# Reordering the drains of two local-attention stages, and the statistics and products around them

## The chip, the cores and the metric

The kernel runs on one core of a Trainium2 chip. The metric is the device time of one execution in microseconds, here the median of several runs. The engines are PE (TensorE), DVE (VectorE), ACT (ScalarE), POOL (GpSimd) and SP (the queue that issues the DMAs).

## The reference

A token mixer, one layer of linear attention and two layers of local attention with a gated feed-forward, all in 32-bit floats. The feed-forward layers see 4096 tokens of 256 channels.

```python
h = einsum('bhid,oi,od->bho', x, weighted_sum, weight)      # images to 4 x 512 tokens
h = concatenate([h, txt], axis=1)                           # 4 x 1024 tokens of 256
h = h + linear_attention(layernorm(h))                      # 16 heads of 64, elu+1, gate
x = layernorm(h)
for l in range(2):
    qkv = shift_token(x) @ wqkv[l]                          # 8 heads of 64
    q, k = rotary_xpos(l2norm(q) * qs, l2norm(k) * ks)
    x = x + local_attention(q, k, v) @ wo[l]                # windows of 128, the one before seen too
    g = layernorm(shift_token(x)) * ln_g + ln_b
    a, b = split(g @ w1[l] + b1[l], 2)
    x = x + (a * gelu(b)) @ w2[l] + b2[l]                   # hidden 682
h = h + x
```

`shift_token` takes the second half of the channels from the token before.

## The kernel before

The 4096 tokens are 32 tiles of 128 (`T = 32`). Every product of 32-bit operands is made of three matmuls (`matmul3`, lines 117 to 119): each operand is split into a rounded high part (a copy by ACT) and the rest (a subtraction by DVE). The program is a sequence of blocks, and at the end of each block all engines meet: `tok_phase`, `attention_phase`, and then `local_phase` and `mlp_phase` for each of two layers. Inside a block each engine has its own list of instructions, written out by hand, and semaphores (`Count`) tie the lists. A `wait(count, n)` holds the whole engine, and everything behind it on that engine.

**Attention.** Four batches of eight tiles. In each batch DVE works out the mean and the variance for the next batch (`norm.variance`, eight small chained instructions, lines 157 to 164), takes the summed key-value products out of PSUM (`take_kv`, line 711), and PE may start the gate projections only when that is done. In batch 0 alone DVE also makes the low part of the output weights in one instruction (line 764), before `take_kv`. At the end of the last batch PE transposes the gated output of the last tile (line 1047), projects window 1 of the first local layer (`qk(1)`, twelve matmuls of 512 columns), makes two output products of 24 matmuls each, and warms itself with ten transposes of the identity (`keep_warm`, line 125). DVE's last work in the block is `bn_stats` on the last two tiles of `H` (line 846).

**Local attention.** A software pipeline over steps `n`: step `n` projects window `n`, scores window `n - 1`, transposes and applies the probabilities of window `n - 2`, and makes the output product of window `n - 3`. Steps 1 to 3 are written out, then a loop, then the drain `T`, `T + 1`, `T + 2`, in which ever less is left. In layer 0, DVE does the variance of the last eight tiles after step 2 and the inverse root (ten small instructions and one more) after step 3 (`between`); ACT waits for it before the loop. In each step ACT makes eight exponentials (line 1317) with their row sums, DVE inverts the sums (line 1453), and POOL multiplies the probabilities by them in two halves of four heads (line 1264). POOL also adds and scales the rotated queries and keys (lines 1272 and 1142).

In the drain, DVE makes the statistics of the first feed-forward group of four tiles in step `T` (`first_stats`) and its eight normalising instructions in step `T + 1` (`first_norm`, lines 1414 and 1416), right after the low part of the attention output (line 1457). PE transposes the result at the end of step `T + 1` (line 1658). Behind the last step DVE scales it by `ln_g` and `ln_b` (line 1529), ACT rounds it (line 1376) and DVE takes the low part (line 1534).

**Feed-forward.** Eight groups of four tiles. For each of six pieces `c` of the hidden layer: `up` (twelve matmuls of 512 columns), gelu on ACT, product `u` on DVE (line 1909), `u_hi` on ACT, `u_lo` on DVE (line 1919), `down`. DVE first has to make the statistics of group 1 (lines 1874 and 1880), for which the shifted channels of group 1 are read back from DRAM. It then works through `hidden(0)`, variance, `hidden(1)`, inverse root, the product of `hidden(2)` and `normalise`, and PE transposes group 1 (line 2010) after that.

Of the kernel before, what the change touches and what calls it, by code (L numbers as in the profile page):

```python
# [12 lines left out]
P = 128  # L13
# [4 lines left out]
T = B * TB  # L18
# [386 lines left out]
def attention_phase(nc, s, mem, K, A):  # L405
# [62 lines left out]
    with nc.Block() as block:  # L468
# [152 lines left out]
        def _(dve):  # L621
# [108 lines left out]
            def batch(b, first, last):  # L730
# [113 lines left out]
            dve.wait_ge(*s.attn_t_done.after(t_full + 6))  # L844
            for w in range(2):
                nc.vector.bn_stats(K.h_stats[:, T - 2 + w], H[:, T - 2 + w])

        @block.tensor
        def _(pe):
# [191 lines left out]
            fill = fills(B - 1, True)[0](STAGES, 0)  # L1041
            pe.wait_ge(*s.attn_o.after(OB * B))
# [6 lines left out]
            qk(1)  # L1049
# [89 lines left out]
def scaled_window(nc, t1, rn, a):  # L1139

    v = t1[:, a].rearrange("p (h d) -> p h d", d=DH)
    return nc.gpsimd.tensor_tensor(v, v, rn[:, a * LH:(a + 1) * LH].unsqueeze(2).to_broadcast([P, LH, DH]), ALU.mult)  # L1142


def local_phase(nc, s, mem, K, A, layer):
# [43 lines left out]
    with nc.Block() as block:  # L1189
# [56 lines left out]
        def _(pool):  # L1246
# [11 lines left out]
            def normalise(t):  # L1258

                pool.wait_ge(*s.inverted.after(t + 1))  # L1260
                for half in range(2):
                    heads = slice(half * LH // 2, (half + 1) * LH // 2)
# [19 lines left out]
            with pool.Fori(2, T // 2) as p:  # L1282
# [4 lines left out]
                nc.gpsimd.tensor_tensor(K.w_l[:, piece], K.w_raw[:, piece], f32(K.w_h[:, piece]), ALU.subtract)  # L1287
                window(2 * p + 1)
            for t in (T - 2, T - 1):
                normalise(t)  # L1290

        @block.scalar
        def _(act):
# [38 lines left out]
            def step(n, r, a, b, c, d, piece=None):  # L1332
# [23 lines left out]
                if a:  # L1356
# [3 lines left out]
                    x_hi(n + 1, 1 - r)  # L1360
                if c:
# [12 lines left out]
            for c in range(KC):  # L1374
                act.wait_ge(*ms.hf.after(c + 1))
                nc.scalar.activation(m_nh[0][:, c], m_hf[:, c], ACT.Copy).then_inc(ms.n_hi.sem, 1)

        @block.vector
        def _(dve):
# [30 lines left out]
            def first_norm():  # L1410

                wait(dve, s.v_full, T)
# [22 lines left out]

            def one_of(n, *steps):
# [3 lines left out]
            def step(n, r, a, b, c, d):  # L1440
# [9 lines left out]
                if c:  # L1450
# [35 lines left out]
                for h in range(LH):  # L1486
# [6 lines left out]
                    if a:  # L1493
# [3 lines left out]
                        else:  # L1497
                            rnorm(LAST).then_inc(s.rnorm.sem, 1)

            late = TB * (B - 1)  # L1500

            def between(n):

                if layer == 0 and n == 2:
                    K.tile_stats(late, T).variance(nc, chain)
                if layer == 0 and n == 3:
                    K.tile_stats(late, T).deviation(nc, chain)
                    nc.vector.scalar_tensor_tensor(nmr[:, late:T], K.l_mean[:, late:T], -1.0, rs[:, late:T], ALU.mult,
                                                   ALU.mult).then_inc(s.stats.sem, 1)
# [17 lines left out]
            for c in range(KC):  # L1527
                dve.wait_ge(*ms.n_t.after(c + 1))
                nc.vector.tensor_scalar(m_hf[:, c], ps[:, c], K.lg[:, layer, c:c + 1], K.lb[:, layer, c:c + 1],
                                        ALU.mult, ALU.add).then_inc(ms.hf.sem, 1)  # L1530
            last_add()
            for c in range(KC):
                dve.wait_ge(*ms.n_hi.after(c + 1))
                nc.vector.tensor_tensor(m_nl[0][:, c], m_hf[:, c], f32(m_nh[0][:, c]), ALU.subtract).then_inc(ms.n_lo.sem, 1)

        @block.tensor
        def _(pe):
# [55 lines left out]
            def step(n, r, a, b, c, d):  # L1593
# [60 lines left out]
                if drain(n, 1):  # L1654
                    pe.wait_ge(*ms.normed.after(1))
                    for c in range(KC):
# [851 lines left out]
```

## Time and profile before

| | us |
|---|---|
| median of 3 runs | 1815.03 |
| lowest and highest | 1814.41, 1819.37 |
| the profiled execution | 1819.65 |
| its span, first to last instruction | 1817.9 |
| PE busy | 1771.5 (97%) |
| DVE busy | 1395.9 (77%) |
| ACT busy | 1003.8 (55%) |
| POOL busy | 528.0 (29%) |

Times in the rows of the trace are microseconds from the first instruction. The local stages lie at about 625 to 1018 (layer 0) and 1221 to 1616 (layer 1). A busy PE is not one at its best, since matmuls overlap: a matmul of 512 columns is listed with 0.39 us, and the next starts 0.23 us after it. The clock column is the granted clock of TensorE as a share of its upper level of 2.4 GHz.

### The profile page before, as it was taken

The numbers are of one execution on the slowest core, as the hardware profiler recorded it, in microseconds if no ns is written. First come the engines' busy times: TensorE is split into PE (matmuls) and PEld (weight loads), VectorE is DVE, ScalarE is ACT, GpSimd is POOL, SyncE is SP. The second block draws the span as 40 slices with busy tenths as digits, with TensorE's granted clock in tenths as the row PEclk, the third lists the DMA queues.
The fourth block names the chain that finished last, engine by engine and source line by source line (L and its number), as shares of the span: only waits on it lengthen the run. The fifth ranks groups of instructions, "written<-read, shape, count | busy, mean of one in ns | idle before, by whom it ended". The sixth has DMA issues, their size and how long they took to land. (4 is left out here: it accounts for less than half of the span.)

```text
span 1817.9 us, 52839 instructions
## 1 busy us (share of the span) xinstructions
PE 1771.5 (97%) x19744; PEld 1554.0 (85%) x19744; DVE 1395.9 (77%) x4325; ACT 1003.8 (55%) x2481; POOL 528.0 (29%) x382
## 2 busy tenths in 40 slices
PE   8999999999999989999999999999999999989998
PEld 7879889889888778888888888888888888888887
DVE  5877877877867788888888687767888888877774
ACT  4443443443434478888887444337777777743333
POOL 0000000000000256666666000016666666611111
PEclk9999999999999999999999999999999999999999
DMA  9200000000020111111111200002111111110011
GB/s 330 83 1 2 2 1 2 1 1 2 1 72 2 40 41 29 26 29 26 29 27 35 100 12 12 1 1 70 28 27 29 27 26 29 32 35 12 6 66 33
DMA packets 64830, 60.44 MB, mean 33 GB/s; under 512 B 16415, under 2 KB 59211, under 8 KB 64718
## 3 DMA queue, kind: packets, MB, share of 16 engines
q1 hardware_dynamic: 64718, 58.88, 10.9%
q8 instruction: 78, 1.28, 0.3%
q14 instruction: 34, 0.28, 0.1%
HBM read 33.95 MB, written 8.39 MB: 23 GB/s over the span
## 5 line engine op out<-in xcount | busy, mean ns | idle before, releaser
L1317 ACT ACTIVATE l_probs<-l_probs,l_negmax 128x192 f32<-128x192 f32 x512 | 225.8, 442 | 86.6 <-DVE l_negmax L1424 86.6
L1142 POOL TENSOR_TENSOR l_t<-l_t,l_rnorm 128x512 f32<-128x512 f32 x128 | 136.1, 1083 | 245.5 <-DVE l_rnorm L1096 245.5
L1264 POOL TENSOR_TENSOR l_probs<-l_probs,l_rowinv 128x768 f32<-128x768 f32 x128 | 185.1, 1466 | 20.1 <-DVE l_rowinv L1453 20.1
L117 PE MATMUL ps<-local_w_hi,l_xT 128*128 128x512 f32 x384 | 158.0, 412 | 1.6 <-PEq L1719 1.1
L1272 POOL TENSOR_TENSOR l_t<-l_t,l_t 128x1024 f32<-128x1024 f32 x62 | 146.9, 2370 | 30.0 <-DVE l_t L1110 18.4
L118 PE MATMUL ps<-local_w_lo,l_xT 128*128 128x512 f32 x384 | 151.6, 395 | 0.0
L119 PE MATMUL ps<-local_w_hi,l_xT 128*128 128x512 f32 x384 | 151.3, 394 | 0.0
L117 PE MATMUL ps<-m_hnT_hi,ffn_w_hi 128*128 128x512 f32 (+1 forms) x352 | 141.0, 400 | 0.0
L512 ACT ACTIVATE attn_exp<-ps 128x512 f32<-128x512 f32 x128 | 76.4, 599 | 116.1 <-PE ps L119 116.1
L119 PE MATMUL ps<-m_hnT_hi,ffn_w_lo 128*128 128x512 f32 (+1 forms) x352 | 138.5, 394 | 0.0
L118 PE MATMUL ps<-m_hnT_lo,ffn_w_hi 128*128 128x512 f32 (+1 forms) x352 | 138.4, 393 | 0.0
L488 POOL MEMSET l_xT<- 128x520 f32 x1 | 0.5, 532 | 463.9 <-PE ps L897 463.9
L1588 PE MATMUL ps<-l_probsT,l_v 128*64 128x64 f32 x2048 | 126.0, 225 | 1.7 <-DVE x L1392 1.0
L1588 PE MATMUL ps<-l_probsT,l_edge 128*64 128x64 f32 x2048 | 123.0, 222 | 0.0
L1105 DVE TENSOR_TENSOR l_t<-ps,rope_c 128x1024 f32<-128x1024 f32 x64 | 78.4, 1225 | 51.6 <-PE ps L1568 46.1
L1834 ACT ACTIVATE m_gelu<-ps,ffn_b 128x512 f32<-128x512 f32 x80 | 55.0, 687 | 110.4 <-PE ps L119 110.4
L1323 ACT ACTIVATE l_probsT<-ps 128x512 f32<-128x512 f32 x192 | 101.1, 598 | 18.9 <-PE ps L1575 14.2
L117 PE MATMUL ps<-attn_w_hi,attn_xT_hi 128*128 128x512 f32 x256 | 107.3, 419 | 3.5 <-issue 1.9
L1588 PEld LDWEIGHTS ps<-l_probsT,l_v 128*64 128x64 f32 x2048 | 104.2, 138 | 6.4 <-ACT l_probsT L1323 2.1
L525 ACT ACTIVATE attn_tanh<-ps 128x512 f32<-128x512 f32 x64 | 38.3, 598 | 121.1 <-PE ps L119 121.1
L1588 PEld LDWEIGHTS ps<-l_probsT,l_edge 128*64 128x64 f32 x2048 | 104.5, 138 | 0.0
L118 PE MATMUL ps<-attn_w_lo,attn_xT_hi 128*128 128x512 f32 x256 | 101.1, 395 | 0.0
(273 smaller groups left out, 5709.1 us busy)
## 6 DMA issues: line engine op xcount, KB each, us to landing
l_edge<-l_v SPq DMA_DIRECT2D x252, 64.0 KB, 2.0
tok_x<-x SPq DMA_DIRECT2D x16, 512.0 KB, 8.0
shifted<-x SPq DMA_DIRECT2D x64, 64.0 KB, 1.5
m_shifted<-shifted SPq DMA_DIRECT2D x16, 256.0 KB, 2.8
out<-x SPq DMA_DIRECT2D x8, 512.0 KB, 3.2
ffn_w_raw<-ffn_w SPq DMA_DIRECT2D x6, 640.0 KB
local_w_raw<-ffn_wqkv SPq DMA_DIRECT2D x4, 768.0 KB, 5.2
tok_base<-attn_base SPq DMA_DIRECT2D x4, 512.0 KB, 9.0
```

Source lines behind the costliest of these rows:

```text
L117: nc.tensor.matmul(out, wh, mh, start=start, stop=False, skip_group_check=True)
L118: nc.tensor.matmul(out, wh, ml, start=False, stop=False, skip_group_check=True)
L119: return nc.tensor.matmul(out, wl, mh, start=False, stop=stop, skip_group_check=True)
L512: nc.scalar.activation(ex[:, at % 2], ps[:, at % 2], ACT.Exp).then_inc(s.attn_exp.sem, 1)
L1105: nc.vector.tensor_tensor(t1[:].rearrange("p a (h d) -> p a h d", d=DH), q, cw, ALU.mult)
L1142: return nc.gpsimd.tensor_tensor(v, v, rn[:, a * LH:(a + 1) * LH].unsqueeze(2).to_broadcast([P, LH, DH]), ALU.mult)
L1264: nc.gpsimd.tensor_tensor(v, v, rinv[:, heads].unsqueeze(2).to_broadcast([P, LH // 2, REACH]), ALU.mult).then_inc(s.normal.sem, 1)
L1272: nc.gpsimd.tensor_tensor(t1[:], t1[:], t2[:], ALU.add).then_inc(s.summed.sem, 1)
L1317: last = nc.scalar.activation(v, v, ACT.Exp, bias=nb[:, h:h + 1], scale=-1.0, accum_out=rsum[:, h:h + 1])
L1323: nc.scalar.activation(pt[:, 4 * k:4 * k + 4].rearrange("p b q -> p (b q)"), ps[:, PT[k]], ACT.Copy).then_inc(s.p_done.sem, 1)
L1588: last = nc.tensor.matmul(ps[e * DH:(e + 1) * DH, OT, pair * P + tokens.start:pair * P + tokens.stop], keys, pt[:, 3 * pair + block, token ...
L1834: nc.scalar.activation(gl[:, c % 2], ps[:, bank + 1], ACT.Gelu, bias=K.b1[:, layer, HC + c:HC + c + 1]).then_inc(s.gelu.sem, 1)
```

## The change

- **Attention, batch 0.** `take_kv` goes ahead of the low part of the output weights.
- **Attention, end.** `qk(1)` goes ahead of the transposes of line 1047. DVE's last `bn_stats` on two tiles leaves the block.
- **Local attention, layer 0, steps 1 to 3.** That `bn_stats` and the variance follow step 1, the seed and two of the three Newton rounds follow step 2, and the third round and the shift follow step 3.
- **Drain, both layers.** In step `T`, behind the scores, DVE inverts the row sums of the first four heads, then runs `first_norm`, then inverts those of the last four; POOL waits for each half by itself. In step `T + 1`, PE begins with the transposes of the normalised group and four warming transposes in place of eight; DVE does the scaling there and the low part behind `add`; ACT rounds ahead of the copies of the transposed probabilities. PE makes half of piece 0 (`up_half`, six matmuls of 512 columns) at the end of step `T + 1` and the other half behind step `T + 2`, whose eight warming transposes go.
- **Feed-forward.** Eight warming transposes go, and group 0 skips `up` of piece 0.

```diff
@@ attention_phase, DVE, batch()
                 early.variance(nc, chain) if last else norm.variance(nc, chain)
+                take_kv(b)
                 if first:
                     dve.wait_ge(*s.attn_wo_hi.after(1))
                     nc.vector.tensor_tensor(wol[:], woraw[:], f32(woh[:]), ALU.subtract).then_inc(s.attn_wo_lo.sem, 1)
-                take_kv(b)
@@ attention_phase, DVE, end
             last_residual(1)
-            dve.wait_ge(*s.attn_t_done.after(t_full + 6))
-            for w in range(2):
-                nc.vector.bn_stats(K.h_stats[:, T - 2 + w], H[:, T - 2 + w])
@@ attention_phase, PE, end
             fill = fills(B - 1, True)[0](STAGES, 0)
+            qk(1)
             pe.wait_ge(*s.attn_o.after(OB * B))
...
-            qk(1)
@@ new
+def up_half(nc, K, out, nh, nl, at):
+
+    for k in range(KC):
+        last = matmul3(nc, out, K.w1_h[:, k, at:at + P], K.w1_l[:, k, at:at + P], nh[:, k], nl[:, k], k == 0, k == KC - 1)
+    return last
@@ local_phase, POOL
-            for t in (T - 2, T - 1):
-                normalise(t)
+            normalise(T - 2)
+            normalise(T - 1, s.half_inverted)
@@ local_phase, ACT, step()
+                if drain(n, 1):
+                    for k in range(KC):
+                        act.wait_ge(*ms.hf.after(k + 1))
+                        nc.scalar.activation(m_nh[0][:, k], m_hf[:, k], ACT.Copy).then_inc(ms.n_hi.sem, 1)
                 if c:
                     for k in range(THIRDS):
                         probs_out(n - 2, k)
@@ local_phase, DVE
+            def half_inverse(half):
+
+                wait(dve, s.exped, 4 * (T - 1) + 2 * half + 2)
+                heads = slice(half * LH // 2, (half + 1) * LH // 2)
+                nc.vector.reciprocal(rinv[:, heads], rsum[:, heads]).then_inc(s.half_inverted.sem, 1)
...
-                if c:
+                if c and not drain(n, 1):
                     wait(dve, s.exped, 4 * (n - 1))
...
                 if drain(n, 1):
-                    first_norm()
+                    for c in range(KC):
+                        dve.wait_ge(*ms.n_t.after(c + 1))
+                        nc.vector.tensor_scalar(m_hf[:, c], ps[:, c], K.lg[:, layer, c:c + 1], K.lb[:, layer, c:c + 1],
+                                                ALU.mult, ALU.add).then_inc(ms.hf.sem, 1)
                 if d and not drain(n, 2):
                     add(n)
+                if drain(n, 1):
+                    for c in range(KC):
+                        dve.wait_ge(*ms.n_hi.after(c + 1))
+                        nc.vector.tensor_tensor(m_nl[0][:, c], m_hf[:, c], f32(m_nh[0][:, c]),
+                                                ALU.subtract).then_inc(ms.n_lo.sem, 1)
...
+                if drain(n, 0):
+                    wait(dve, s.normal, 2 * (T - 1))
+                    half_inverse(0)
+                    first_norm()
+                    half_inverse(1)
...
             def between(n):
 
-                if layer == 0 and n == 2:
-                    K.tile_stats(late, T).variance(nc, chain)
-                if layer == 0 and n == 3:
-                    K.tile_stats(late, T).deviation(nc, chain)
...
+                    if n == 1:
+                        for w in range(2):
+                            done = nc.vector.bn_stats(K.h_stats[:, T - 2 + w], H[:, T - 2 + w])
+                        chain(done)
+                        norm.variance(nc, chain)
+                    val = norm.dev[:, :, 0]
+                    if n == 2:
+                        rsqrt(nc, chain, norm.rstd, norm.tmp, val, 1)
+                        newton(nc, chain, norm.rstd, norm.tmp, val)
+                    if n == 3:
+                        newton(nc, chain, norm.rstd, norm.tmp, val)
@@ local_phase, PE, step()
                 if drain(n, 1):
-                    keep_warm(nc, K, XT, 8)
-                if drain(n, 2):
-                    keep_warm(nc, K, V, 8)
+                    pe.wait_ge(*ms.normed.after(1))
+                    for c in range(KC):
+                        for j in range(4):
+                            last = nc.tensor.transpose(ps[:, c, j * P:(j + 1) * P], m_hn[:, j, c * P:(c + 1) * P], K.ident[:])
+                        last.then_inc(ms.n_t.sem, 1)
+                    keep_warm(nc, K, XT, 4)
...
                 if drain(n, 1):
-                    pe.wait_ge(*ms.normed.after(1))
...
+                    pe.wait_ge(*ms.n_lo.after(KC))
+                    pe.wait_ge(*s.ffn_lo.after(SPLITS))
+                    up_half(nc, K, ps[:, 0], m_nh[0], m_nl[0], 0)
 
             schedule(pe, step)
+            up_half(nc, K, ps[:, 1], m_nh[0], m_nl[0], HC * P).then_inc(ms.ag_full.sem, 1)
             keep_warm(nc, K, V, 8)
@@ mlp_phase, PE
-            keep_warm(nc, K, 4, 8)
-            group(0, 0, False)
+            group(0, 0, False, skip=True)
```

The scaling, the rounding and the low part that stood behind the last step go from there, and POOL's last weight subtraction gets a semaphore (`ffn_lo`) for PE to wait on.

## Rows read from the trace of the kernel before

**Rows 1.** The page, costliest groups: busy us, mean ns of one, idle before.
```profile
L1317 ACT ACTIVATE l_probs<-l_probs,l_negmax 128x192 f32<-128x192 f32 x512 | 225.8, 442 | 86.6 <-DVE l_negmax L1424 86.6
```
**Rows 2.** Windows: length, busy of each engine (x count), granted clock, DMA.
```profile
665.00:669.00 4.00, 4.00 (x18) 3.32 (x17) 3.20 (x5) 2.16 (x5) 2.68 (x2) 0.57 0.15 37
126.00:130.00 4.00, 4.00 (x20) 2.76 (x21) 2.89 (x13) 0.60 (x2) 0.00 (x0) 0.57 0.00 0
1010.00:1014.00 4.00, 4.00 (x22) 3.82 (x20) 3.34 (x9) 1.12 (x2) 1.39 (x1) 0.57 0.14 33
1605.00:1609.00 4.00, 3.05 (x30) 2.74 (x31) 3.66 (x9) 1.60 (x3) 1.71 (x2) 1.00 0.14 33
```
**Rows 3.** Timeline of DVE, attention batch 0: start us, us, engine, line.
```profile
122.26 2.29 DVE L764 TENSOR_TENSOR attn_wo_lo<-attn_wo_raw,attn_wo_hi 128x2048 fp32r<-128x2048 f32 x1
...
131.24 0.82 DVE L700 TENSOR_TENSOR attn_out<-ps,attn_z 128x640 f32<-128x640 f32 x1
```
**Rows 4.** Timeline of PE, attention batch 0, first gate product; idle before in brackets.
```profile
125.33 0.47 PE L117 MATMUL ps<-attn_w_hi,attn_xT_hi 128*128 128x512 f32 x1 [1.90 <-issue]
```
**Rows 5.** Timeline of the end of attention, PE and DVE.
```profile
614.02 1.16 PE L1047 MATMUL ps<-ident,attn_out 128*128 128x128 f32 x8 [1.16 <-DVE attn_oT_lo L825]
...
616.57 1.28 DVE L825 TENSOR_TENSOR attn_oT_lo_last<-ps,attn_oT_hi_last 128x512 fp32r<-128x512 f32 x2
...
625.05 0.75 DVE L846 BATCH_NORM_STATS2 h_stats<-h 128x6 f32<-128x256 f32 x2
```
**Rows 6.** Timeline of DVE and POOL at the end of layer 0's feed-forward.
```profile
1212.61 1.38 DVE L1919 TENSOR_TENSOR m_u_lo<-m_u,m_u_hi 128x512 fp32r<-128x512 f32 x1 [0.70 <-ACT m_u_hi L1795]
...
1213.40 1.75 POOL L1763 TENSOR_TENSOR local_w_lo<-local_w_raw,local_w_hi 128x512 fp32r<-128x512 f32 x1
```
**Rows 7.** Timeline of steps 2 to 4 of layer 0: POOL, DVE, PE.
```profile
645.52 2.04 POOL L1142 TENSOR_TENSOR l_t<-l_t,l_rnorm 128x512 f32<-128x512 f32 x2 [3.68 <-DVE l_rnorm L1096]
...
645.70 0.90 DVE L159 TENSOR_TENSOR l_dev<-h_stats,l_mean 128x16 f32<-128x16 f32 x1
...
658.47 0.16 DVE L130 TENSOR_SCALAR l_rstd<-l_dev 128x8 int32<-128x8 int32 x1
...
662.00 0.17 DVE L1508 SCALAR_TENSOR_TENSOR l_shift<-l_mean,l_rstd 128x8 f32<-128x8 f32 x1
...
663.93 0.38 PE L117 MATMUL ps<-local_w_hi,l_oT_hi 128*128 128x256 f32 x1 [2.07 <-DVE l_oT_lo L1457]
```
**Rows 8.** Timeline of the drain of layer 1: DVE and POOL.
```profile
1603.53 0.20 DVE L1453 RECIPROCAL l_rowinv<-l_rowsum 128x8 f32<-128x8 f32 x1 [1.89 <-ACT l_probs L1317]
...
1603.82 2.89 POOL L1264 TENSOR_TENSOR l_probs<-l_probs,l_rowinv 128x768 f32<-128x768 f32 x2 [8.23 <-DVE l_rowinv L1453]
...
1605.29 1.50 DVE L1416 TENSOR_SCALAR m_hn<-m_shifted,m_mean,m_rstd 128x128 f32<-128x128 f32 x1
...
1608.00 0.33 DVE L1416 TENSOR_SCALAR m_hn<-m_shifted,m_mean,m_rstd 128x128 f32<-128x128 f32 x1
```
**Rows 9.** Timeline of the same drain: PE and ACT.
```profile
1604.76 0.39 PE L117 MATMUL ps<-local_w_hi,l_oT_hi 128*128 128x256 f32 x1 [2.22 <-DVE l_oT_lo L1457]
...
1612.55 0.36 PE L117 MATMUL ps<-local_w_hi,l_oT_hi 128*128 128x256 f32 x1
...
1613.01 1.35 ACT L1376 ACTIVATE m_hnT_hi<-m_hnT 128x512 fp32r<-128x512 f32 x2 [1.48 <-DVE m_hnT L1529]
```
**Rows 10.** Timeline from layer 1's drain into its feed-forward: DVE and PE.
```profile
1616.22 1.06 PE L125 MATMUL ps<-ident 128*128 128x128 f32 x8 [1.11 <-PEq L1189]
...
1619.28 0.87 DVE L1880 BATCH_NORM_STATS2 m_stats<-m_shifted 128x6 f32<-128x128 f32 x4 [1.81 <-DMA m_shifted<-shifted]
...
1620.90 0.75 DVE L1909 SCALAR_TENSOR_TENSOR m_u<-ps,ffn_b,m_gelu 128x512 f32<-128x512 f32 x1 [0.74 <-ACT m_gelu L1834]
...
1631.49 1.09 PE L2010 MATMUL ps<-ident,m_hn 128*128 128x128 f32 x8 [0.31 <-DVE m_hn L1888]
```
**Rows 11.** The same handover in layer 0, DVE.
```profile
1026.83 0.75 DVE L1909 SCALAR_TENSOR_TENSOR m_u<-ps,ffn_b,m_gelu 128x512 f32<-128x512 f32 x1 [0.87 <-ACT m_gelu L1834]
```

More of the change, by code:

```diff
@@ L1256, in _, with normalise @@
                 nc.gpsimd.memset(kt[:, :, 1], 0.0).then_inc(s.kt_set.sem, 1)
-            def normalise(t):
-                pool.wait_ge(*s.inverted.after(t + 1))
+            def normalise(t, half_inverted=None):
+                if half_inverted is None:
+                    pool.wait_ge(*s.inverted.after(t + 1))
                 for half in range(2):
+                    if half_inverted is not None:
+                        pool.wait_ge(*half_inverted.after(half + 1))
                     heads = slice(half * LH // 2, (half + 1) * LH // 2)
@@ L1286, in _ @@
                 piece = bass.ds((FW // SPLITS) * (p - 2), FW // SPLITS)
[L1287 removed]
+                nc.gpsimd.tensor_tensor(K.w_l[:, piece], K.w_raw[:, piece], f32(K.w_h[:, piece]),
+                                        ALU.subtract).then_inc(s.ffn_lo.sem, 1)
                 window(2 * p + 1)
[L1289 to L1290 removed]
+            normalise(T - 2)
+            normalise(T - 1, s.half_inverted)
         @block.scalar
@@ L1373, in _ @@
             schedule(act, step, pieces=True, loop=lambda: layer == 0 and act.wait_ge(*s.stats.after(1)))
-            for c in range(KC):
-                act.wait_ge(*ms.hf.after(c + 1))
-                nc.scalar.activation(m_nh[0][:, c], m_hf[:, c], ACT.Copy).then_inc(ms.n_hi.sem, 1)
         @block.vector
@@ L1410, in first_norm @@
             def first_norm():
-                wait(dve, s.v_full, T)
+                dve.wait_ge(*s.v_full.after(T))
                 for j in range(4):
@@ L1526, in _ @@
             schedule(dve, step, rebase, between=between)
[L1527 to L1530, printed above, removed]
             last_add()
-            for c in range(KC):
-                dve.wait_ge(*ms.n_hi.after(c + 1))
-                nc.vector.tensor_tensor(m_nl[0][:, c], m_hf[:, c], f32(m_nh[0][:, c]), ALU.subtract).then_inc(ms.n_lo.sem, 1)
         @block.tensor
@@ L1654, in step @@
                 if drain(n, 1):
-                    pe.wait_ge(*ms.normed.after(1))
-                    for c in range(KC):
-                        for j in range(4):
-                            last = nc.tensor.transpose(ps[:, c, j * P:(j + 1) * P], m_hn[:, j, c * P:(c + 1) * P], K.ident[:])
-                        last.then_inc(ms.n_t.sem, 1)
+                    pe.wait_ge(*ms.n_lo.after(KC))
+                    pe.wait_ge(*s.ffn_lo.after(SPLITS))
+                    up_half(nc, K, ps[:, 0], m_nh[0], m_nl[0], 0)
             schedule(pe, step)
+            up_half(nc, K, ps[:, 1], m_nh[0], m_nl[0], HC * P).then_inc(ms.ag_full.sem, 1)
             keep_warm(nc, K, V, 8)
@@ L2057, in turned_t, with group @@
                     last.then_inc(ls.qk_t.sem, 1)
-            def group(g, r, tail=True, final=False):
+            def group(g, r, tail=True, final=False, skip=False):
                 ahead = final and AHEAD
@@ L2062, in group @@
                 for c in range(C):
-                    up(g, r, c)
+                    if not (skip and c == 0):
+                        up(g, r, c)
                     if ahead and c == 0:
```

8 lines of the change are left out of this document (6 added, 2 removed).

## The prediction

> **What bounds the kernel now.** I read the page first. PE is busy for 1771.5 of the 1817.9 us of the span (97%), so only a few stretches are left in which a change can give anything: where PE stands still, and where it works at half its clock. The costliest group of ACT is the exponentials [rows 1], 512 of 442 ns; that number comes back in the drain. Then I read the windows for the clock. Three stretches of some 4 us have a granted clock of 0.57, which is the lower level of 1.2 GHz for most of the stretch: at 665 us, at 126 us, and in layer 0's drain at 1010 us; layer 1's drain has 1.00 [rows 2]. The change touches all of these places. What half speed costs in such a stretch I take from the pitch of PE's matmuls inside and outside it (0.43 against 0.23 us): about half of 3 to 3.6 us, 1.3 to 1.6 us. Last I read the timelines around each edit. The sum is made against the profiled execution (1819.65, some 1.8 us more than its span); it lies 4.6 us above the median of 1815.03, so I apply the difference to the median. 0.3% is 5.4 us, about what runs of this kernel tell from no change.
>
> **A. `take_kv` first in batch 0.** DVE's subtraction takes 2.29 us until 124.55 [rows 3], then comes `take_kv`, and PE's first gate product starts at 125.33 after 1.90 us idle [rows 4]. With the order turned PE need not wait: at most 1.90 back, and at most 1.6 more if the clock does not fall after a shorter gap, 3.5 in all. But what follows the subtraction on DVE (the other query features) starts when it did, since the two pieces only change places. PE gets ahead and waits for those features; DVE's output of the first tile at 131.24 [rows 3] can come at most 1.5 us sooner, since the deviation ahead of it ends later than the features. I take −1.5; bounds 0 and −3.5.
>
> **B. End of attention.** PE waits 1.16 us before the transposes of line 1047 [rows 5]. With `qk(1)` (twelve matmuls at a pitch of 0.23, 2.8 us) ahead of them, this wait is covered. But the first output product needs DVE's low part, which was made by 617.85 from transposes that now come 1.6 us later; product 0 then starts only 0.1 to 0.2 us sooner. The `bn_stats` that leave cost 0.75 and ended the block at 625.80 [rows 5], and PE's warming ended 0.3 us before. So the block ends about 0.25 sooner. Bounds: 0, and −1.9 if both were to come off whole (1.16 + 0.75).
>
> **C. Late statistics, layer 0.** The ten small instructions and the shift of step 3 ran from 658.47 to 662.17, and PE behind them waited 2.07 us until 663.93 [rows 7]. Seven of them leave; two of those were the 0.9-us ones that POOL's two 1-us multiplications held up (as at 645.70 in step 2, where line 159 lasts 0.90 while POOL's line 1142 runs, a 0.17-us kind of instruction [rows 7]). So they do not leave for nothing: whatever stands first behind the scores waits for POOL, in every step. Step 1 gets `bn_stats` (0.75 as above) and eight small ones with the same hold-up: DVE's list there ends about 2.2 us later than before, of which its idle time takes 1.1, so step 2 starts about 1.0 later. Step 2 has seven instead of eight (+0.8 left behind it). Step 3 has four, of which the same two are held up: 0.16 + 0.2 + 0.9 + 0.97 and so on, and it ends about 0.5 before the old time. PE's wait of 2.07 shrinks by that and by PE's own later arrival, to about 1. I take −0.5 for the wait, and −1.6 for the half-speed stretch at 665 [rows 2], whose cause I read as that wait (it is PE's longest just before). Bounds: +0.8 (POOL's hold-up moves into step 1 on the path) and −3.3.
>
> **D. The drains, times of layer 1.** *Row sums.* DVE's scores end about 1601.65 (1.89 us idle before line 1453 at 1603.53 [rows 8]). The eight exponentials end just before that, at a pitch of 0.44 [rows 1], so the first four are done at 1603.5 − 4 × 0.44 = 1601.75. The half inverse (0.20, the whole one's price, bound from above) ends about 1602.0 and POOL's first half (2.89 for both, 1.45 each [rows 8]) starts at 1602.1, 1.7 sooner than at 1603.82. *The port.* DVE's normalising instructions and POOL's multiplication hold each other up: line 1416 at 1605.29 lasts 1.50 instead of 0.33 [rows 8] while POOL's second half runs. And the one that waited comes next: line 1919 lasts 1.38 beside POOL, and then POOL's line 1763 lasts 1.75, having waited in its turn [rows 6]. So I expect one normalising instruction, POOL's half (to 1603.65), and then DVE's other seven at a pitch of 0.26, to about 1605.5. Only then comes the second half inverse, and POOL's second half runs from 1605.7 to 1607.15, against 1606.71 before: the halves start sooner, and end later by 0.45.
>
> The Trainium skill, "SBUF — State Buffer", section "Who interferes with whom", says that DVE and GpSimd share one pair of ports as an exclusive lock held for the instruction. The rows on lines 1416 and 1919 agree. It does not say who gets the lock next; if always DVE did, its eight would run first, which is the rival R1 below.
>
> *PE.* It went idle at 1602.54 and waited 2.22 us for the low part, until 1604.76 [rows 9]; warming stood before that. Now nothing covers it: the transposes of the group need `first_norm`'s end. They start at about 1605.6 (4.2 us idle), 0.9 us of transposes and 0.4 of four warming ones, and the output product of step T + 1 starts at 1606.9 instead of 1604.76, +2.15. Behind it: the probabilities' transposes and values until about 1612.85, waiting for POOL's second half; half of piece 0 (six matmuls, 1.4 us) covers the chain ACT, DVE to the last product, which starts at about 1614.4 instead of 1612.55 [rows 9]. DVE's scaling (1.5, the idle of ACT's rounding [rows 9]) and ACT's rounding (1.35) now lie before the copies of the probabilities, which they put off by part of their length; that is in the 1.85. Then the second half of piece 0 and warming: the block ends about 1618.5 instead of at 1616.22 [rows 10], where the transposes of 1.06 begin on release. +2.25.
>
> *What comes back in the feed-forward.* Its piece 0 is done: 2.8 us of PE and eight transposes (1.06). But that isn't what PE waits for there. DVE's chain sets it: the statistics wait 1.81 for a DMA and start at 1619.28; line 1909 starts at 1620.90, having waited 0.74 for gelu; and PE waits for normalised group 1 until 1631.49 [rows 10], 10.6 later. The DMA is issued on release, so `u` starts 3.95 us after release now (4.68 less 0.74), and everything behind it to 1631.49 keeps its length. The saved `up` gives only the 0.74 in layer 1, and 0.87 in layer 0 [rows 11]. Layer 1: +2.25 − 0.74 = +1.5.
>
> Layer 0 is the same, with two differences: 0.13 more comes back, and its drain already had a stretch at half speed [rows 2] that cost 1.26 and is gone unless a new one comes. +1.5 − 0.13 − 1.26 = +0.1. Together +1.65 at full clock. After 4.2 us idle in each I expect a new stretch in each, since 2.07 and 1.90 us were followed by one [rows 7, 4], while 2.22 in layer 1's drain was not [rows 9, 2]. 1.2 each: +2.4. D = +4.05; bounds −2 (below, R1 and more) and +16 (R5).
>
> The Trainium skill, "TensorE: Matmul & The Clock Gate", section "What's actually happening", calls the low clock the default that activity lifts. By that the longer idle speaks against this change, and more than by my 2.4 us if the work behind it has gaps. The rows show both levels after gaps of 2 us, so they leave it open.
>
> **The sum.** −1.5 − 0.25 − 0.5 − 1.6 + 1.65 + 2.4 = +0.2, on the median 1815.2. A change with many parts of which the drains give back what the others save. Its own range is 1812 to 1818.5 (−3, +3.3, from the bounds of A and C taken one at a time). Chance 0.50.
>
> **Rivals.**
> - R1: DVE keeps the port and runs all eight normalising instructions before POOL's first half. They end at about 1604.0 instead of 1605.5, PE starts 1.5 sooner, and both drains gain 1.5 or slightly more: −3.1, 1812.1. For it: both orders of waiting occur; against: rows 6, where the waiting engine goes next. 0.13.
> - R2: the clock stays at its upper level in both drains, as after 2.22 us in layer 1: −2.4, 1812.8. Against: the idle is nearly twice as long. 0.15.
> - R3: both, and A at −2.4 or more: −6.2 or more, around 1808.8. 0.10.
> - R4: the feed-forward's `u` isn't bound by the DMA, since its issue or landing turns out earlier, and `u` starts 2.3 us after release: −1.65 per layer, 1811.9. Against: 1.81 of idle that ends with the DMA [rows 10]. 0.07.
> - R5, the other side: in a drain with 4.2 us idle PE resumes at 1.2 GHz and stays there until the handover, since each short burst is followed by a wait. Some 10.7 us of matmuls then take twice as long, of which about 8 us come through to the end: two drains +16, less the 2.4 counted, +13.8: 1829. One drain alone: 1822. It decides from the point where a drain loses over 3.8 us. Against: each half-speed stretch of before ended within 4 us. 0.05.
>
> **How the numbers follow.** The likeliest case gives 1815.2. The range 1809 to 1820 takes in R1, R2, R4 and the middle of R3, and upward C's bound with a longer stretch in each drain; R5 and the rest of R3 and the likeliest case's tails stay out. Faster by over 0.3% (below 1809.6) needs R3 or two of the others together: 0.13. Slower (above 1820.5) is R5 and a little of the likeliest case's tail: 0.06. Same: 0.81.
>
> **What would show each step.** A: PE's gap before the first gate product gone, and waits for query features instead; the clock at 126 above 0.57. B: no wait at the transposes, the block ending within 0.5 us of before. C: DVE's instructions of about 0.9 in step 1, step 2 late by 1 us, PE's wait in step 3 near 1 us and the clock at 665 near 1. D: POOL's halves apart with DVE's instructions between them, the first of these about 1.5 long; PE idle for about 4.2 us, then half clock for a few us; the product of step T + 1 some 2.1 late; the feed-forward's `u` 3.95 us after release with no wait for gelu. The prediction is wrong if DVE's eight instructions are done by 1604, if the clock does not follow the idle time, or if the saved `up` is worth more than 0.9 us a layer.

## The result and the profile after

The changed kernel takes 1820.8 us (median of 20 runs, 1818.43 to 1823.75), the kernel before, on as many runs, 1817.54 (1814.41 to 1820.61). The ratio is 1.0018 with a 95% interval of 1.0011 to 1.0025: 3.3 us slower, 2.0 to 4.5. Forecast were 1815.2 us and +0.2. The profiled execution of the changed kernel is of its fastest (1818.43 us), that of before was of its slower ones (1819.65), so the two profiles by themselves say 1.2 us faster. The medians of 20 runs decide: against them the profile of before is 2.1 us slow and that of the changed kernel 2.4 us fast.

The page, span and busy time of each engine:

```profile
span 1816.6 us, 52764 instructions
PE 1764.6 (97%) x19704; PEld 1546.6 (85%) x19704; DVE 1397.2 (77%) x4327; ACT 1003.9 (55%) x2481; POOL 528.2 (29%) x382
```

**Parts A to C.** The timelines of DVE and PE in attention batch 0, at the end of attention, and of steps 1 and 3 of layer 0 (PE after DVE, parts marked by dots):

```profile
121.84 0.76 DVE L711 COPY attn_kv<-ps 128x260 f32<-128x260 f32 x2
122.52 2.28 DVE L765 TENSOR_TENSOR attn_wo_lo<-attn_wo_raw,attn_wo_hi 128x2048 fp32r<-128x2048 f32 x1
...
129.31 0.82 DVE L700 TENSOR_TENSOR attn_out<-ps,attn_z 128x640 f32<-128x640 f32 x1
...
122.85 0.40 PE L117 MATMUL ps<-attn_w_hi,attn_xT_hi 128*128 128x512 f32 x1
...
613.55 1.03 PE L1045 MATMUL ps<-ident,attn_out 128*128 128x128 f32 x8
...
633.01 0.97 DVE L159 TENSOR_TENSOR l_dev<-h_stats,l_mean 128x16 f32<-128x16 f32 x1
...
661.01 0.38 PE L117 MATMUL ps<-local_w_hi,l_oT_hi 128*128 128x256 f32 x1 [0.67 <-DVE l_oT_lo L1471]
```

`take_kv` is ahead, the gate product has no wait, and the first tile's output starts 1.93 us sooner than at 131.24 [rows 3]; 0.43 of that were there before batch 0 began, so A is worth 1.5 in this pair. The transposes at 613.55 have lost their wait [rows 5]. In step 1 line 159 is now one of the held-up 0.97-us instructions, and PE's wait in step 3 has gone from 2.07 [rows 7] to 0.67.

**The clock**, the two early windows of [rows 2] and three that matter now (length, busy of PE, PE's loads, DVE, ACT and POOL, granted clock, DMA):

```profile
126.00:130.00 4.00, 2.41 (x46) 1.72 (x46) 3.56 (x15) 0.97 (x2) 0.00 (x0) 1.00 0.00 0
665.00:669.00 4.00, 4.00 (x134) 3.73 (x132) 3.86 (x24) 2.77 (x10) 1.27 (x1) 1.00 0.08 20
1005.00:1009.00 4.00, 3.35 (x30) 3.35 (x31) 3.15 (x9) 1.26 (x2) 1.47 (x1) 1.00 0.14 33
1024.00:1028.00 4.00, 3.63 (x9) 2.91 (x10) 3.03 (x11) 1.21 (x2) 0.00 (x0) 0.57 1.03 390
1602.00:1606.00 4.00, 4.00 (x26) 4.00 (x25) 1.88 (x3) 1.26 (x2) 1.23 (x1) 0.68 0.14 33
```

Both early stretches at 1.2 GHz are gone, and so is that at 1010 us [rows 2]. One has come at 1024, in the feed-forward of layer 0, where none was looked for, and one in layer 1's drain.

**Part D, drain of layer 0**, timelines of DVE, POOL and PE (DVE's scores end at 1002.03):

```profile
1002.24 0.18 DVE L1448 RECIPROCAL l_rowinv<-l_rowsum 128x4 f32<-128x4 f32 x1 [0.21 <-ACT l_probs L1325]
1002.34 0.31 DVE L1422 TENSOR_SCALAR m_hn<-x,m_mean,m_rstd 128x128 f32<-128x128 f32 x1
1002.57 1.49 DVE L1424 TENSOR_SCALAR m_hn<-m_shifted,m_mean,m_rstd 128x128 f32<-128x128 f32 x1
...
1005.25 0.34 DVE L1424 TENSOR_SCALAR m_hn<-m_shifted,m_mean,m_rstd 128x128 f32<-128x128 f32 x1
1005.51 0.17 DVE L1448 RECIPROCAL l_rowinv<-l_rowsum 128x4 f32<-128x4 f32 x1
...
1002.50 1.48 POOL L1271 TENSOR_TENSOR l_probs<-l_probs,l_rowinv 128x768 f32<-128x768 f32 x1 [6.53 <-DVE l_rowinv L1448]
1005.76 1.47 POOL L1271 TENSOR_TENSOR l_probs<-l_probs,l_rowinv 128x768 f32<-128x768 f32 x1 [1.78 <-DVE l_rowinv L1448]
...
1005.65 1.09 PE L1646 MATMUL ps<-ident,m_hn 128*128 128x128 f32 x8 [3.74 <-DVE m_hn L1424]
```

This is the forecast picture of [rows 8, 9] turned: one normalising instruction, a second that lasts 1.49 because POOL's first half runs, then six at a pitch of 0.26, then the second inverse, and POOL's halves 1.78 us apart. PE waits 3.74 us.

**The handover.** DVE in layer 0 of the kernel before, from the release (the moment at which all engines have met and the next block starts; the MEMSET is DVE's first instruction behind it) to the statistics of group 1:

```profile
1022.22 0.27 DVE L1986 MEMSET m_u_rest<- 128x256 f32 x1 [0.40 <-PEq L1189]
1025.08 0.87 DVE L1880 BATCH_NORM_STATS2 m_stats<-m_shifted 128x6 f32<-128x128 f32 x4 [1.69 <-DMA m_shifted<-shifted]
```

DVE and PE in the changed kernel, layer 0 and then layer 1:

```profile
1018.55 0.27 DVE L2017 MEMSET m_u_rest<- 128x256 f32 x1 [2.17 <-PEq L1193]
...
1022.65 0.87 DVE L1911 BATCH_NORM_STATS2 m_stats<-m_shifted 128x6 f32<-128x128 f32 x4 [2.92 <-DMA m_shifted<-shifted]
1023.56 0.75 DVE L1940 SCALAR_TENSOR_TENSOR m_u<-ps,ffn_b,m_gelu 128x512 f32<-128x512 f32 x1
...
1024.37 0.79 PE L117 MATMUL ps<-m_hnT_hi,ffn_w_hi 128*128 128x512 f32 x1 [2.71 <-DVE m_u L1940]
...
1615.95 0.27 DVE L2017 MEMSET m_u_rest<- 128x256 f32 x1 [2.17 <-PEq L1193]
...
1618.78 0.87 DVE L1911 BATCH_NORM_STATS2 m_stats<-m_shifted 128x6 f32<-128x128 f32 x4 [1.65 <-DMA m_shifted<-shifted]
1619.69 0.75 DVE L1940 SCALAR_TENSOR_TENSOR m_u<-ps,ffn_b,m_gelu 128x512 f32<-128x512 f32 x1
...
1620.49 0.50 PE L117 MATMUL ps<-m_hnT_hi,ffn_w_hi 128*128 128x512 f32 x1 [1.45 <-DVE m_u L1940]
```

As forecast nothing waits for gelu any more, and in layer 1 `u` starts 3.74 us behind the release instead of 4.60. In layer 0 it starts 5.01 behind it: the shifted rows of group 1 land 1.2 us later than in the profile of before (idle 2.92 against 1.69 above, and 1.81 in layer 1 [rows 10]). PE, which has only piece 1 left to do, stands 2.71 us, and behind that comes the stretch at 1.2 GHz.

### The profile page after: what moved, and what is told of

The parts are those of the page before. It is cut to its first block and busy times, and to the rows that moved or that the text cites. A ratio compares the mean times of both kernels' runs of the same rounds, so it can differ in the third digit from the quotient of the medians.

```text
span 1816.6 us, 52764 instructions
## 1 busy us (share of the span) xinstructions
PE 1764.6 (97%) x19704; PEld 1546.6 (85%) x19704; DVE 1397.2 (77%) x4327; ACT 1003.9 (55%) x2481; POOL 528.2 (29%) x382
## 3 DMA queue, kind: packets, MB, share of 16 engines
q8 instruction: 77, 1.26, 0.3%
## 5 line engine op out<-in xcount | busy, mean ns | idle before, releaser
L1826 ACT ACTIVATE m_u_hi<-m_u 128x512 fp32r<-128x512 f32 x80 | 50.6, 632 | 93.8 <-DVE m_u L1940 92.8
```

## The experiments

Ten variants and the two unchanged kernels ran, each in five rounds beside runs of the kernel before on the same chip (experiments 1 to 4, 5 to 8 and 9 to 12 on one chip each). Ratios are to the kernel before, with 95% intervals; 0.001 is 1.8 us. Differences between two variants are differences of their ratios.

**1. Parts A, B and C without D.** The changed kernel with every edit of the drains and of the feed-forward taken back.

> Parts A, B and C without D (the drains and the feed-forward as before). Theory 1: the half-speed stretches at 126 and 665 us that the profile of before shows are in only some of its executions, so against the median A and C give little more than their waits: A about -0.2, B -0.3, C -0.5, together -1 us (ratio 0.9994), and at most -4 against an execution that has both stretches. Theory 2: before nearly always has both stretches, and the three parts give what the pair of profiles shows, -1.5 - 0.3 - 2.1 = -3.9 us (0.9979); then D costs 7 us.

Measured: 0.9985 (0.9976 to 0.9994), -2.7 us, with an interval from -4.4 to -1.1. It lies between the two theories and settles neither; 2, 9 and 10 say more. Its profile has neither early stretch, but one in each drain, that of layer 1 included, where the two of before have none.

**2. Part D alone.** The other half.

> Part D alone (both drains and the start of the feed-forward as in the change, the rest as before). Theory 1: +4 to +4.5 us (1.0023): about 1.6 us a layer from the later start of the transposes less what comes back, and the rest from half-speed stretches after 3.7 us of idle PE. Theory 2: +7 us (1.0039). In the profile, in either: 3.7 us of idle PE ahead of the transposes of the group in each drain, and a wait of 1.4 to 2.7 us in the feed-forward for the first u.

Measured: 1.0037 (1.0024 to 1.0051), +6.7 us. Nearer to theory 2: D costs more than was counted, and the three parts pay for about two fifths of it. The DVE and PE rows of the handover in layer 1 (the release, the rows, `u`, and PE behind it) show one place:

```profile
1621.58 0.27 DVE L2011 MEMSET m_u_rest<- 128x256 f32 x1 [2.17 <-PEq L1196]
...
1625.67 0.88 DVE L1905 BATCH_NORM_STATS2 m_stats<-m_shifted 128x6 f32<-128x128 f32 x4 [2.91 <-DMA m_shifted<-shifted]
1626.58 0.75 DVE L1934 SCALAR_TENSOR_TENSOR m_u<-ps,ffn_b,m_gelu 128x512 f32<-128x512 f32 x1
...
1627.38 0.50 PE L117 MATMUL ps<-m_hnT_hi,ffn_w_hi 128*128 128x512 f32 x1 [2.72 <-DVE m_u L1934]
```

The rows are late here too, in the layer in which they were in time in the first profile. So their landing varies between executions.

**3 and 4. Both kernels again, unchanged.**

> The kernel before, unchanged, for a second profile. Theory 1: 1.000, and the half-speed stretches lie elsewhere or are fewer than in the first profile (32, 126, 665 and 1010 us); the clock in the stretch 126 to 130 or 665 to 669 us is 1.00 in at least one of them. Theory 2: both stretches are there again.

Measured: 1.0000 (0.9991 to 1.0009). Expected by theory 1 was a missing stretch; both are there (windows of this run):

```profile
126.00:130.00 4.00, 4.00 (x43) 2.99 (x45) 2.54 (x12) 0.94 (x2) 0.00 (x0) 0.69 0.00 0
663.00:667.00 4.00, 3.45 (x16) 3.16 (x17) 3.55 (x5) 3.43 (x8) 2.68 (x3) 0.68 0.14 33
1009.00:1013.00 4.00, 3.77 (x19) 3.77 (x20) 4.00 (x10) 0.11 (x1) 2.18 (x2) 0.57 0.14 33
```

> The changed kernel, unchanged, for a second profile (the first is of the fastest of 20 runs). +0.18%, the ratio measured. Theory 1: the profile shows half-speed stretches in more places than the two of the first (1024 and 1602 us), among them one in each drain or behind it. Theory 2: the stretches are the same two, and the time is lost in a wait that the first profile did not show.

Measured: 1.0018 (1.0009 to 1.0028). More stretches than in the first profile, as theory 1 has it, in both drains and in the feed-forward:

```profile
1005.00:1009.00 4.00, 3.10 (x15) 3.10 (x16) 3.13 (x8) 0.98 (x3) 1.47 (x1) 0.50 0.14 33
1009.00:1013.00 4.00, 3.71 (x23) 3.47 (x22) 1.62 (x3) 1.51 (x4) 0.00 (x0) 0.70 0.06 16
1028.00:1032.00 4.00, 4.00 (x14) 3.27 (x13) 3.03 (x11) 1.40 (x3) 0.00 (x0) 0.57 1.02 385
1604.00:1608.00 4.00, 3.40 (x19) 3.41 (x20) 2.73 (x7) 1.26 (x2) 1.47 (x1) 0.66 0.14 33
```

The one in layer 0's drain is about twice as long as any of before. The mean granted clock was 0.9952 in the 20 runs of the changed kernel and again in the 11 of this experiment; in 26 runs of the kernel before beside these 11 it was 0.9969.

**5. Normalising ahead of the half inverse.**

```diff
                 if drain(n, 0):
                     wait(dve, s.normal, 2 * (T - 1))
-                    half_inverse(0)
                     first_norm()
+                    half_inverse(0)
                     half_inverse(1)
```

> The changed kernel with the eight normalising instructions of the drain ahead of the first half inverse (POOL starts its first half after them). Against the changed kernel, which is at +0.18% of before. Theory 1 (the order on DVE costs the drain its time: POOL's first half holds the second normalising instruction up by 1.2 us, and nothing covers PE): PE's idle time ahead of the transposes falls from 3.74 to about 2.3 us in both drains, POOL's second half ends within 0.2 us of where it did, and the kernel gains 1.1 us a layer, -2.2, plus what the clock gives back; +0.06% of before or less. Rival: the transposes of the probabilities wait for POOL all the same, the gain of the idle time is lost again behind the output product of step T + 1: no change.

Measured: 0.9992 (0.9983 to 1.0001); 4.7 us less than the changed kernel's 1.0018. POOL's two halves and PE's transposes in layer 0's drain:

```profile
1004.23 2.90 POOL L1271 TENSOR_TENSOR l_probs<-l_probs,l_rowinv 128x768 f32<-128x768 f32 x2 [8.28 <-DVE l_rowinv L1448]
...
1004.12 1.09 PE L1646 MATMUL ps<-ident,m_hn 128*128 128x128 f32 x8 [2.23 <-DVE m_hn L1424]
```

POOL ends at 1007.13, where it ended at 1007.23 with the halves: inverting them apart brings POOL nothing, as its second half waits for DVE all the same. PE waits 1.5 us less, and both drains ran at 1.00 in this execution. The gain is 1.5 a layer at full clock (the table below), above the 1.1 expected. The rest, 1.7 us, fits the clock, whose mean rose from 0.9952 to 0.9968, but nothing here separates it.

**6. The shifted rows of group 1 read in the drain**, behind the value product of the last window.

```diff
@@ local_phase, SP
             own_edge(T - 1, 1)
+            sp.dma_start(K.mlp_t[layer][0][:, 1], A.scratch[4 * P:8 * P, :].rearrange("(j p) c -> p j c", p=P)
+                         ).then_inc(ms.sh_in[1].sem, 16)
             store(T // 2 - 1, 0)
@@ mlp_phase, SP
-            shifted(0, 0)
```

> The changed kernel with the shifted rows of group 1 read in the drain of the local block (behind the value product of the last window), not on the feed-forward's start. Theory 1 (with piece 0 done ahead, the first u waits for these rows alone): u starts 2.3 to 2.4 us after release in both layers, against 3.75 in layer 1 and 5.0 in layer 0; PE's waits of 1.4 and 2.7 us ahead of piece 2 go; -1.4 and -2.7, together -4 us; 0.9996 to 1.0000 of before. Rival: gelu with its table load ends about when the rows land, and only 0.7 us a layer come of it: -1.4, +0.10% of before.

Measured: 0.9998 (0.9989 to 1.0007), 3.6 us less than the changed kernel. DVE behind the release in layer 0:

```profile
1020.79 0.27 DVE L2018 MEMSET m_u_rest<- 128x256 f32 x1 [2.17 <-PEq L1193]
...
1023.01 0.75 DVE L1941 SCALAR_TENSOR_TENSOR m_u<-ps,ffn_b,m_gelu 128x512 f32<-128x512 f32 x1 [0.27 <-ACT m_gelu L1866]
```

`u` starts 2.22 us behind the release, in both layers, and waits for gelu only 0.27. PE's wait ahead of piece 2 is gone in both. Theory 1 holds.

**7. Both edits together.**

> The two edits together (normalising instructions first, rows of group 1 early). They lie in different stretches and should add: -6.2 us against the changed kernel by theory 1, -2.9 us against before (0.9984). By the rivals together: -1.4 against the changed kernel, +0.10% of before.

Measured: 0.9969 (0.9958 to 0.9980), 5.6 us faster than before, 8.9 less than the changed kernel. They add: 4.7 and 3.6 make 8.3.

**8. The changed kernel without the halves of piece 0.** The feed-forward makes piece 0 as before, and the warming transposes are back.

> The changed kernel without the two halves of piece 0 in the drain (the feed-forward makes piece 0 and the eight warming transposes there and behind step T + 2 as before). Theory 1 (the halves cost PE 1.4 us in the drain that the feed-forward can't use, since its first u waits for the rows): the block ends 1.4 us or more sooner, u starts 4.7 us after release, with a wait for gelu again; net -0.7 us in layer 1 and -1 to -2 in layer 0, +0.04 to +0.09% of before. Rival (the prediction's term: the first half only covers the wait for the last low part, and the second comes back): within 0.5 us of the changed kernel, +0.18%.

Measured: 1.0012 (1.0003 to 1.0021), 1.1 us less than the changed kernel; the intervals overlap, so it leans to theory 1 and doesn't settle it alone. In this version SP issues the read of the shifted rows 0.7 us behind the release, not on it. The row of PE's last product in the drain of layer 0 shows what the first half covered:

```profile
1016.84 0.38 PE L117 MATMUL ps<-local_w_hi,l_oT_hi 128*128 128x256 f32 x1 [0.40 <-DVE l_oT_lo L1471]
```

A wait of 0.40: so much is all that 1.4 us of matmuls had covered there.

**9 and 10. A alone, C alone.**

> Part A alone (take_kv first in attention batch 0). Theory 1 (the wait and the half-speed stretch behind it go together, and all executions have the wait): -1.5 us against before (0.9992), PE's idle 1.9 us at 123 us gone and the clock at 1.00 there. Theory 2 (the stretch is in two of three executions only, and without it DVE's chain holds the first output back all the same): -1.0 us (0.9994), with 0.2 us left where the stretch was absent.

Measured: 0.9991 (0.9982 to 1.0000), -1.6 us. The wait is gone, the clock is 1.00 at 123 to 131 us. The interval (-3.3 to 0) holds both theories; experiments 2 and 10, whose profiles have the wait without the stretch, speak for the premise of theory 2.

> Part C alone (late statistics spread over steps 1 to 3, with bn_stats out of the attention block). Prediction's terms: -0.5 for the wait and -1.6 for the stretch at 665 us; -2.1 us (0.9988). Rival: the stretch comes back at another place in the same steps (PE still waits 0.7 us there, and 1.4 in step 1), only the wait is gained: -0.7 us (0.9996).

Measured: 0.9985 (0.9976 to 0.9994), -2.7 us: the prediction's terms, not the rival. Windows of this run, at batch 0, where its code is that of before, and around step 3:

```profile
126.00:130.00 4.00, 3.98 (x77) 2.85 (x79) 3.56 (x15) 1.49 (x3) 0.00 (x0) 1.00 0.00 0
662.00:666.00 4.00, 4.00 (x73) 3.54 (x75) 3.93 (x9) 3.20 (x7) 2.37 (x1) 1.00 0.20 48
666.00:670.00 4.00, 4.00 (x96) 3.61 (x88) 3.76 (x28) 3.07 (x14) 0.50 (x1) 1.00 0.11 25
```

The stretch in batch 0 is missing here though `take_kv` is late. In the four profiles with the old order it was there in two, in the ten with the new order in none; that at 665 was there in all four with the old statistics, and in none of the other ten.

**11. Warming transposes in the wait**, on top of 7.

```diff
                 if drain(n, 1):
+                    keep_warm(nc, K, XT, 16)
                     pe.wait_ge(*ms.normed.after(1))
```

> The version with normalising first and early rows, and sixteen warming transposes of the identity in the 2.2 us in which PE waits for the normalised group in each drain. Theory (the clock falls behind PE's idle time in about half of the drains that have 2.2 us of it, at 1.4 to 2.5 us each): the stretch at half speed is in neither drain, -1 to -2 us against the version without (0.9969 of before), so 0.9959 to 0.9964. Rival: 16 transposes overrun the wait (0.11 us each, 1.8 of 2.2), or the clock falls for another reason: no change or +0.3.

Measured: 0.9958 (0.9944 to 0.9971), 7.6 us faster than the kernel before: the best of all. All its five runs are faster than all seven of experiment 7 (1809.9 to 1813.03), but on another chip. PE in layer 0's drain:

```profile
1001.59 1.97 PE L125 MATMUL ps<-ident 128*128 128x128 f32 x16
...
1003.90 1.09 PE L1649 MATMUL ps<-ident,m_hn 128*128 128x128 f32 x8 [0.34 <-DVE m_hn L1426]
```

The clock is at its upper level in both drains and both feed-forwards; it is low only behind PE's last matmul, at the end of the program. Its five runs lie within 0.7 us (1809.06 to 1809.72).

**12. The version of 7 without the halves of piece 0.**

> The version with normalising first and early rows, without the halves of piece 0 in the drain. Theory 1 (once the rows are there, the first u waits for gelu of piece 0, so that the halves are worth what they take out of the feed-forward): u starts 4.6 us after release against 2.2, the block ends 1.4 us sooner; net +1 us a layer, +2 (0.9980 of before). Rival (the halves are no gain in any setting): within 0.5 us of 0.9969.

Measured: 0.9982 (0.9973 to 0.9991), 2.4 us more than with them. The intervals (to 0.9980 with them, from 0.9973 without) just overlap; the trace speaks for theory 1. DVE behind the release in layer 0:

```profile
1016.10 0.27 DVE L2017 MEMSET m_u_rest<- 128x256 f32 x1 [0.94 <-PEq L1193]
...
1020.71 0.75 DVE L1940 SCALAR_TENSOR_TENSOR m_u<-ps,ffn_b,m_gelu 128x512 f32<-128x512 f32 x1 [2.66 <-ACT m_gelu L1865]
```

`u` waits 2.66 us for gelu. So the halves are worth something only when the rows are there; when the rows are late, they buy a wait for a DMA.

**The drains side by side.** From the timelines of DVE: from the end of the scores of step T to the release (start of the MEMSET), and from there to `u`, each in layer 0 and layer 1, in us.

| | scores to release | release to `u` |
|---|---|---|
| before | 15.90, 14.66 | 4.61, 4.60 |
| before, again | 15.89, 14.64 | 4.61, 4.61 |
| A alone | 15.91, 14.64 | 4.97, 4.60 |
| C alone | 15.89, 14.64 | 4.94, 4.61 |
| A, B, C without D | 15.62, 15.90 | 4.60, 4.60 |
| changed | 16.52, 17.92 | 5.01, 3.74 |
| changed, again | 19.05, 18.08 | 5.00, 3.73 |
| D alone | 18.02, 19.02 | 5.45, 5.00 |
| changed, no halves | 17.72, 17.88 | 4.81, 4.60 |
| changed, rows early | 18.99, 18.13 | 2.22, 2.22 |
| changed, normalising first | 15.02, 15.02 | 3.71, 5.12 |
| both | 15.02, 16.58 | 2.21, 2.22 |
| both, warm | 15.02, 15.02 | 2.22, 2.22 |
| both, no halves | 13.79, 15.39 | 4.61, 4.61 |

## Why the prediction was wrong

**A and B: borne out.** A -1.5 forecast, -1.6 measured alone (interval -3.3 to 0, so the size isn't settled), and -1.5 in the first pair. B: local attention of layer 0 starts 0.3 us sooner in the first pair than the start of batch 0 and A explain, 0.25 forecast.

**C: borne out.** -2.1 forecast, -2.7 measured alone. DVE's hold-up by POOL moved into step 1 as described, and in the first pair C gave 2.1: PE's wait fell by 1.4, of which half was lost again in the steps ahead, and the stretch went. That A, B and C together gave only 2.7 where their parts make 4.5 lies within the intervals. But the sum was made against an execution that had both early stretches, 4.6 us above the median to which it was applied, and the one at 126 us is in only two of four such profiles: the 3.85 us booked for A to C could come short for that reason alone.

**D, the drain: the mechanism right, two sizes off, which cancel by luck.** POOL and DVE alternate on the port in the order of the forecast: the second normalising instruction lasts 1.49 us against 1.50, and PE waits 3.74 us against 4.2. By the Trainium skill ("SBUF — State Buffer", section "Who interferes with whom") the port is held for the whole instruction; the 1.49-us instruction agrees. Rival R1, in which DVE runs its eight first, did not happen by itself, and experiment 5 made it happen and was worth what R1 said, 1.5 a layer (16.52 to 15.02 at full clock). At full clock the drain is 1.88 us longer (16.52 against 14.64), 2.25 was forecast. The stretches cost more than the 1.2 each that I took: the drains of the changed code are 16.52 without one, some 18.0 with a short one (1.5) and 19.0 with a long one (2.5). The mean of the eight drains of the full changed code (changed twice, D alone, rows early) is 18.22, that of the ten old ones 15.37: +2.85 a layer, 5.7 together, where the forecast terms of the drains make 5.64 (twice 2.25, plus 2.4, less 1.26). A stretch came behind 3.74 us of idle in nine drains of ten (those of experiment 8 counted), as R5's argument and the forecast have it, and R2 is out. R5 itself, a clock that stays low until the handover, did not occur; the longest stretch costs 2.5, not 8. (Its +13.8 should read +13.6: 16 less 2.4.) The Trainium skill, "TensorE: Matmul & The Clock Gate", section "What's actually happening", calls the low clock the default that activity lifts. The profile of experiment 11 agrees: filled with warming transposes, the gap had no stretch in either drain. It is weak evidence by itself, since the unfilled gaps of 2.23 us (experiments 5, 7 and 12) had one in only two drains of six.

**The step that failed: what comes back in the feed-forward.** "The saved `up` gives only the 0.74 in layer 1, and 0.87 in layer 0": the forecast took the landing time of the shifted rows from one profile as fixed. They took that time in eight of ten old handovers (idle of 1.68 to 1.87 in front of the statistics; 2.88 and 2.85 in the two others), but in only two of the six of the changed kernel (two profiles) and of D alone (1.64 and 1.65); the four others had 2.91 to 3.36. With the old order gelu was the last to come, so a late row cost 0.35; with piece 0 done ahead nothing covers it, and a late row costs 1.3. The slack that I booked as a gain was the cover. Where the rows were in time the term held (4.60 to 3.74, 0.87 back). On the mean of those six `u` starts 4.66 us behind the release (4.60 with the two of experiment 5), against 4.68 on the ten old ones in the table: next to nothing came back, where 1.61 had been booked for both layers. The whole blocks say the same: from the release to the first projection of layer 1, and from the release to the end of the program, the means of the six together are 0.2 us longer than the old ones. R4, in which the transfer isn't the bound, did not occur, and experiment 6 confirms from the other side that it is: with the rows early `u` starts at 2.22 behind the release. Added up with the other terms as forecast, +0.2 becomes +1.8; 3.3 (2.0 to 4.5) is measured. The rest of 1.5 isn't placed: D alone measures 6.7 (4.4 to 9.3) against 5.7 by this account, A to C together 2.7 (1.1 to 4.4) against the 3.85 forecast, and both lie within the intervals.

**The base.** The time of 1815.2 stood on a median of three runs, 1815.03. On 20 runs it is 1817.54. 2.5 of the 5.6 us by which the time was missed are that, and the range should have reached over it.

**Open: what makes the rows late.** The other loads of the feed-forward of layer 0 aren't the cause by themselves, since layer 1 has none and had late rows twice (experiments 2 and 5). The views of the transfers show a companion. In experiment 5, layer 1, with late rows, and then in the changed kernel, layer 1, with rows in time (GB/s in 40 slices of 1609 to 1616 us; packets, MB and share of 16 engines of queue q8; the shifted rows with their time from issue to landing):

```profile
GB/s 179 3 0 0 0 0 0 0 0 0 0 0 181 108 26 108 313 331 319 322 331 336 322 231 21 20 20 21 20 18 20 20 0 0 0 0 0 0 0 0
q8 instruction: 1, 0.02, 1.2%
m_shifted<-shifted SPq DMA_DIRECT2D x2, 256.0 KB, 4.4
...
m_shifted<-shifted SPq DMA_DIRECT2D x2, 256.0 KB, 3.1
```

Every handover of the fourteen profiles has one packet of queue q8, a fetch of instructions, near it. It lies 0.5 to 2 us behind the release in all seven handovers in which the rows were issued on the release and landed after 4.0 to 4.6 us, and 3 us or more ahead of the release in all eleven in which they were issued on it and landed after 2.8 to 3.2. The packet takes 1.2% of 16 engines for 7 us, which is 1.3 us of one engine, and the end of the late transfer runs at 20 GB/s, about a sixteenth of the 336 before. So an estimate from these rows is that the part of the rows that goes through one DMA engine stands behind the fetch. That is a coincidence in time, not an experiment, and one case speaks against a simple rule: in layer 0 of experiment 8, where the rows were issued 0.7 us later, the fetch fell right behind the issue and they landed after 3.2. What places the fetch isn't known either. It fell into the first 2 us in two of ten old handovers and in seven of fourteen of the changed code with the halves of piece 0; the rows were late in two of ten and in five of the eight of these whose rows were read on release. Whether that is the new code or chance isn't settled.

## What to carry to other kernels

Work that is moved ahead of a wait gives only what the next-latest releaser leaves. That one should be read from several executions, since a cover of 0.7 us may be hiding a transfer that is at times 1.3 us late; and then it is the transfer that should be moved first (here 3.6 us, against about 1 lost by moving the matmuls alone).

Two engines that share a port take turns: putting a short chain on which PE waits ahead of a long POOL operation cost POOL nothing here, and starting POOL earlier cost the chain 1.5 us.

A gap of PE at the end of a block is priced with the half-speed stretch behind it (1.25 to 2.5 us), and filling it with warming transposes was worth 2.0 us (0.9969 to 0.9958, with intervals that overlap).

## What the runs showed of the chip

Stretches at 1.2 GHz behind idle PE: in nine of ten drains with 3.74 us idle, in eight of sixteen with 2.2, in none of two with 0.34. In the feed-forward behind waits of 2.7 to 3.2 us in five of five, behind 1.4 us in none of three. Idle time isn't all that decides: the same code in the same place (2.22 us in the old drain) had one in layer 0 in all five profiles and in layer 1 in one.

DVE and POOL on their shared port: an instruction of DVE of 0.33 us lasts 1.49 when it starts beside POOL's of 1.48, and the one that waited goes next.

A read of shifted rows (256 KB) that is issued near the release landed after 2.6 to 3.2 us in fifteen handovers without an instruction fetch in the 2 us behind the release, after 4.0 to 4.6 in eight of nine with one, and after 3.2 in the ninth.

Executions of the kernel before differ mostly by the clock: one thousandth of mean granted clock went with about 1 us (the 11 runs of experiment 3: 1816.33 us at 0.999, 1821.03 at 0.994). It isn't so in every kernel: in experiment 6 a run at 0.995 took 1816.64 us and one at 0.998 took 1816.43.
